# Seventeen groups of edges compared in place of fifteen, layer-norm sums by bn_stats, and earlier first loads in a graph network kernel

## What is computed

```python
h = maximum(layernorm(x), 0)
# three SAGE layers: agg = mean over edges of h[src]; agg @ Wl.T + b + h @ Wr.T, relu after the first two
x = x + sage3(h)
h = maximum(layernorm(x), 0)
messages = gelu((h[src] + edge_attr) @ We1 + be1) @ We2 + be2
aggregated = segment_sum(messages, dst)
x = x + (gelu(((1 + eps) * h + aggregated) @ Wu1 + bu1) @ Wu2 + bu2)
```

## Time and profile before

| | us |
|---|---|
| median of 3 runs (lowest to highest) | 895.88 (895.14 to 899.03) |
| the profiled execution | 895.96 |
| its span, first to last instruction | 894.0 |
| TensorE busy (share of span) | 822.2 (92%) |
| VectorE busy | 662.0 (74%) |
| GpSimd busy | 390.0 (44%) |
| ScalarE busy | 325.3 (36%) |
| mean granted TensorE clock, share of full | 0.974 |

### The profile page before, as it was taken

How to read it: one execution, slowest core, us unless ns; L and a number is a source line. 1 busy time by engine, 2 the same in 40 slices (tenths; PEclk the granted TensorE clock), 3 DMA queues, 4 the chain that set the end, 5 groups by cost and what they waited for, 6 DMA issues and landing times.

```text
span 894.0 us, 14740 instructions
## 1 busy us (share of the span) xinstructions
PE 822.2 (92%) x4894; PEld 626.2 (70%) x4894; DVE 662.0 (74%) x1807; ACT 325.3 (36%) x575; POOL 390.0 (44%) x451
## 2 busy tenths in 40 slices
PE   4987999999999999999699999999899989999995
PEld 1743555555687887778467898887787777888783
DVE  8599999998355445454599988869777877787761
ACT  3576677776155555454111112111112121112111
POOL 1000000000022222232577777777777777777772
PEclk9969999999999999999699999999999999999997
DMA  4300010100000000000673444444434434443421
GB/s 132 86 3 13 3 14 13 15 3 17 9 1 0 1 1 13 12 23 13 149 228 95 126 134 148 135 134 148 127 97 148 136 89 147 135 132 90 136 77 38
DMA packets 37388, 67.50 MB, mean 76 GB/s; under 512 B 14625, under 2 KB 24828, under 8 KB 37180
## 3 DMA queue, kind: packets, MB, share of 16 engines
q1 hardware_dynamic: 25916, 43.15, 16.0%
q0 software_dynamic: 11392, 23.35, 9.6%
HBM read 63.18 MB, written 3.30 MB: 74 GB/s over the span
## 4 chain that ended last, share of the span: by engine, by line
PE 46%; POOL 25%; DVE 15%; issue 10%; DMA 2%; ACT 1%; SPq 0%; ACTq 0%; POOLq 0%; DVEq 0%
POOL f_adj L648 25%; PE f_ps L1332 15%; PE f_ps L1325 9%; DVE f_select L919 4%; PE f_ps L1209 3%; PE f_ps L1387 3%; PE f_ps L1202 3%; PE f_ps L1429 2%; PE f_ps L1299 2%; PE f_ps L1261 1%; PE f_ps L1373 1%; DVE f_region L700 1%; DVE f_region L698 1%; DVE f_adj L1033 1%; DVE f_region L704 1%
## 5 line engine op out<-in xcount | busy, mean ns | idle before, releaser
L648 POOL DMA_INDIRECT f_adj<-table,f_by_edge x356 | 338.3, 950 | 109.8 <-issue 107.0
L919 DVE TENSOR_SCALAR f_select<-f_ps 128x512 fp32r<-128x512 f32 x375 | 230.5, 679 | 3.6 <-PE f_ps L1387 3.1
L1387 PE MATMUL f_ps<-f_select,f_pair 125*128 125x512 f32 x750 | 206.4, 416 | 15.9 <-DVE f_select L919 15.8
L633 POOL CAST f_wide<-f_adj 125x500 fp32r<-125x500 uint8 (+1 forms) x70 | 40.4, 577 | 362.3 <-ACT f_adj L1065 216.4
L1387 PEld LDWEIGHTS f_ps<-f_select,f_pair 125*128 125x128 f32 x750 | 135.6, 190 | 64.3 <-DVE f_select L919 32.2
L1188 ACT ACTIVATE f_adj<-f_adj 128x512 f32<-128x512 f32 (+1 forms) x90 | 56.3, 626 | 326.2 <-DVE f_adj L1033 320.1
L1332 PE MATMUL f_ps<-f_wide,f_pair 125*128 125x500 f32 (+1 forms) x700 | 162.6, 385 | 1.5 <-DVE f_wide L757 0.6
L1065 ACT CAST f_adj<-f_ps 128x500 f32 x213 | 126.1, 592 | 55.7 <-PE f_ps L1209 40.9
L1332 PEld LDWEIGHTS f_ps<-f_wide,f_pair 125*128 125x128 f32 x700 | 122.2, 189 | 33.6 <-issue 6.2
L1429 PEld LDWEIGHTS f_ps<-f_adj 128*128 128x128 f32 x984 | 123.8, 192 | 17.6 <-DVE f_adj L894 8.1
L1429 PE MATMUL f_ps<-f_adj 128*128 128x94 f32 (+20 forms) x984 | 123.8, 271 | 8.8 <-ACT f_adj L1188 8.8
(11 more groups left out here) (147 smaller groups left out, 692.4 us busy)
## 6 DMA issues: line engine op xcount, KB each, us to landing
f_region<-in_edge_attr_T SPq DMA_DIRECT2D x34, 768.0 KB
f_adj<-table,f_by_edge POOLq DMA_INDIRECT x356
f_src_rows<-in_src_row SPq DMA_DIRECT2D x15, 256.0 KB, 4.8
f_adj<-inv SPq DMA_DIRECT2D x1, 1562.5 KB, 7.2
table<-f_region SPq DMA_DIRECT2D x6, 250.0 KB
out<-f_xT SPq DMA_DIRECT2D x6, 250.0 KB, 2.4
f_rcntT<-inv SPq DMA_DIRECT2D x5, 250.0 KB, 3.7
f_xT<-in_xT SPq DMA_DIRECT2D x1, 812.5 KB, 6.2
```

Of the source, the lines that this page charges most:

```text
L648: pool.indirect_dma_start(out=rows[:, r % RW, j * D:(j + 1) * D], out_offset=None, in_=table, in_offset=bass.IndirectOffsetOnAxis(ap=table ...
L919: ins = dve.tensor_scalar(select[:, u % SELECT, :], offset, float(b * NP - CENTRE), None, ALU.is_equal)
L1387: ins = pe.matmul(z_columns(g), chosen[0:NP, p, b, :], select[0:NP, u % SELECT, :], start=b == 0 and p == 0, stop=b == NB - 1 and p == 1, ...
```

## The change

- Seventeen groups are picked (`SHARES`), the gaps between them become six, twice seven.
- The first layer norm's sums come from VectorE: 25 bn_stats in slots 10 to 16 (`statistics0`), joined by five short operations (`join0`) in slot 16, root in slot 17, inversion in slot 20. The products and squares on TensorE and ScalarE go.
- x is loaded ahead of xT, and its loads and the table's stores are cut at partition 112 (`EVENLY`); xT comes later, in one piece, and `dst_tiles` early, straight to where it is used.
- The first edge_attr (three groups) goes to a part of `rcntT` after the fourth table store, the first source row to another part after the fifth; both were issued after the seventh. The rotation of later loads is shifted by one.
- In VectorE's iteration g, the comparisons for g+1 come first, before the one-hots of g+2 and the add of g. On the other engines the order stays.

```diff
-        self.SHARES = 15
+        self.SHARES = 17
...
-            self.put("cent0", 8 + 2 * c, c)
-            self.put("square0", 8 + 2 * c, c)
-            self.put("var0", 10 + 2 * c, c)
+            self.put("stats0", 10 + c, c)
...
-        std = 10 + 2 * s.NC
+        std = 10 + s.NC
+        self.put("join0", std - 1, 0)
         self.put("std0", std, 0)
         self.put("inv0", std + 3, 0)
...
+    EVENLY = NP // 16 * 16
...
         def edge_tiles(g, lo, hi):
             at_tile = s.tile(g) - s.tile(g // PER * PER)
+            if g < PER:
+                return rcntT[:, (at_tile + lo) * P:(at_tile + hi) * P]
             return ea[:, g // PER % EA, (at_tile + lo) * P:(at_tile + hi) * P]
...
-            sp.dma_start(xT[:, 0:HALF * NP], t["xT"][:, 0:HALF * NP]).then_inc(xT_in[0], 16)
-            sp.dma_start(xT[:, HALF * NP:N], t["xT"][:, HALF * NP:N]).then_inc(xT_in[1], 16)
-            sp.dma_start(x_rows[0:NP, 0:HALF, :], t["x"][0:HALF * NP, :].rearrange("(b p) d -> p b d", p=NP)
-                         ).then_inc(x_in[0], 16)
-            sp.dma_start(x_rows[0:NP, HALF:NB, :], t["x"][HALF * NP:N, :].rearrange("(b p) d -> p b d", p=NP)
-                         ).then_inc(x_in[1], 16)
-            sp.wait_ge(x_in[1], 16)
+            for i, (lo, hi) in enumerate(((0, HALF), (HALF, NB))):
+                rows_in = t["x"][lo * NP:hi * NP, :].rearrange("(b p) d -> p b d", p=NP)
+                for p0, p1 in ((0, EVENLY), (EVENLY, NP)):
+                    sp.dma_start(x_rows[p0:p1, lo:hi, :], rows_in[p0:p1, :, :]).then_inc(x_in[i], 16)
+            sp.wait_ge(x_in[1], 32)
...
+            sp.dma_start(xT[:, :], t["xT"]).then_inc(xT_in, 16)
+            sp.dma_start(dst_abs[:, :].bitcast(I32), t["dst_tiles"]).then_inc(dst_tile_in, 16)
...
             for c in range(NC):
...
+                for p0, p1 in ((0, EVENLY), (EVENLY, NP)):
+                    sp.dma_start(rows_to[p0:p1, :, :], rows_from[p0:p1, :, :]).then_inc(rows_out[c % 2], 16)
+                if c == 3:
+                    sp.wait_ge(agg_kept, 2 * NC + 4)
+                    sp.dma_start(rcntT[:, 0:FIRST_EA], t["edge_attr_T"][:, 0:FIRST_EA]).then_inc(ea_first, 16)
+                if c == 4:
+                    sp.wait_ge(agg_kept, 2 * NC + 6)
+                    sp.dma_start(first_src, src_columns(0)).then_inc(src_first, 16)
-            load_edges(0)
-            for i in range(2):
-                sp.dma_start(src_rows[:, i, :], src_columns(i)).then_inc(src_in[i], 16)
-            sp.dma_start(dst_tile[:, :], t["dst_tiles"]).then_inc(dst_tile_in, 16)
+            sp.dma_start(src_rows[:, 1, :], src_columns(1)).then_inc(src_in[1], 16)
...
             load_edges(1)
+            load_edges(2)
...
+            def statistics0(c):
+                for b in s.blocks(c):
+                    if b in (0, HALF):
+                        dve.wait_ge(x_in[b // HALF], 32)
+                    ins = dve.bn_stats(stats0[:, b, :], x_rows[0:NP, b, :])
+                ins.then_inc(stats0_ready, 1)
+
+            def join0():
+                dve.wait_ge(stats0_ready, NC)
+                dve.tensor_tensor(gap0, stats0[:, :, 1], stats0[:, :, 4], ALU.subtract).then_inc(joined0, 1)
+                dve.tensor_tensor(spread0, stats0[:, :, 2], stats0[:, :, 5], ALU.add).then_inc(joined0, 1)
+                dve.tensor_tensor(twice0, stats0[:, :, 1], stats0[:, :, 4], ALU.add).then_inc(joined0, 1)
+                dve.wait_ge(joined0, 3)
+                dve.scalar_tensor_tensor(out=gap0, in0=gap0, scalar=D / 4, in1=gap0, op0=ALU.mult, op1=ALU.mult
+                                         ).then_inc(joined0, 1)
+                dve.wait_ge(joined0, 4)
+                dve.tensor_tensor(spread0, spread0, gap0, ALU.add).then_inc(joined0, 1)
...
                 if g < G:
+                    for i, b in s.selections(g + 1):
+                        select_sources(i, b)
                     if g + OH_AHEAD < G:
                         window_onehots(g + OH_AHEAD)
                     if g not in s.picked:
...
                         dve.tensor_tensor(pre[:, r % PR, 0:w], z_group(g), rows[:, r % RW, 0:w],
                                           ALU.add).then_inc(pre_ready, 1)
-                    for i, b in s.selections(g + 1):
-                        select_sources(i, b)
...
             def root0():
-                act.wait_ge(var0_ready, NC)
-                act.activation(std0[0:NP, :], ps[0:NP, VAR0_PS:VAR0_PS + NB], ACT.Sqrt, bias=col["epsln"][0:NP, 0:1]
+                act.wait_ge(joined0, 5)
+                act.activation(std0[0:NP, :], spread0, ACT.Sqrt, bias=col["epsln"][0:NP, 0:1], scale=1.0 / D
                                ).then_inc(std0_ready, 1)
...
             def mix(g):
-                pe.wait_ge(ea_in[g // PER % EA], 16 * (g // PER // EA + 1))
+                u = g // PER
+                if u == 0:
+                    pe.wait_ge(ea_first, 16)
+                else:
+                    pe.wait_ge(ea_in[u % EA], 16 * ((u + 1) // EA))
```

More of the change, by code:

```diff
@@ L327, in fast_path @@
         rstdT, o = carve(flat, o, (N,), F32)
-        dst_tile, o = carve(flat, o, (FT,), I32)
         uT = rcntT
+        FIRST_EA, FIRST_SRC = PER * T * P, s.cols(4)[0]
+        first_src = rcntT[:, FIRST_SRC:FIRST_SRC + T * P].bitcast(I32)
+        assert FIRST_EA <= s.cols(4)[0] and FIRST_SRC + T * P <= s.cols(5)[1]
         select = placed_at("select", [P, SELECT, T * P], F32R, third)
@@ L340, in fast_path @@
             sem("idx_in"), sem("first_in"), sem("dst_in"), sem("small_in"), sem("sage_in"), sem("gine_in"))
-        x_in, xT_in = [sem(f"x_in{i}") for i in range(2)], [sem(f"xT_in{i}") for i in range(2)]
+        x_in, xT_in = [sem(f"x_in{i}") for i in range(2)], sem("xT_in")
         idx_rest, dst_rest, blank = sem("idx_rest"), sem("dst_rest"), sem("blank")
@@ L345, in fast_path @@
         onehots, nexts_in, summed, kept = sem("onehots"), sem("nexts_in"), sem("summed"), sem("kept")
-        centred0, squared0, var0_ready, std0_ready, scaled0, normed0, hT_kept = (
-            sem("centred0"), sem("squared0"), sem("var0_ready"), sem("std0_ready"), sem("scaled0"), sem("normed0"),
-            sem("hT_kept"))
+        stats0_ready, joined0, std0_ready, scaled0, normed0, hT_kept = (
+            sem("stats0_ready"), sem("joined0"), sem("std0_ready"), sem("scaled0"), sem("normed0"), sem("hT_kept"))
+        stats0 = work[0:NP, 0, 0:6 * NB].rearrange("p (b i) -> p b i", i=6)
+        gap0, spread0, twice0 = (work[0:NP, 1, i * NB:(i + 1) * NB] for i in range(3))
         centred, squared, var_ready, std_ready, inverted, normed = (
@@ L367, in fast_path @@
                                                         sem("selected"))
-        src_in = [sem(f"src_in{i}") for i in range(2)]
-        ea_in = [sem(f"ea_in{i}") for i in range(EA)]
+        src_in, src_first = [sem(f"src_in{i}") for i in range(2)], sem("src_first")
+        ea_in, ea_first = [sem(f"ea_in{i}") for i in range(EA)], sem("ea_first")
         gathered = [sem(f"gathered{i}") for i in range(RW)]
@@ L583, in _ @@
             for g in range(END):
-                if g % PER == PER - 1 and g // PER + EA < UNITS:
+                if g % PER == PER - 1 and EA < g // PER + EA < UNITS:
                     sp.wait_ge(z_ready, g + 1)
@@ L850, in _ @@
                     edge_keys(HEAD, NT)
+                for c in plan.due("stats0", slot):
+                    statistics0(c)
+                for _ in plan.due("join0", slot):
+                    join0()
                 for _ in plan.due("inv0", slot):
@@ L903, in source_offsets @@
                     dve.wait_ge(placed, 2)
[L904 removed]
+                if i == 0:
+                    dve.wait_ge(src_first, 16)
+                else:
+                    dve.wait_ge(src_in[i % 2], 16 * ((i + 1) // 2))
                 if i == 0:
@@ L1147, in _ @@
                     root0()
-                for c in plan.due("square0", slot):
-                    square0(c)
                 for c in plan.due("square", slot):
@@ L1211, in sum_group @@
                 ins.then_inc(summed, 1)
-            def centre0(c):
-                if c == 0:
-                    pe.wait_ge(xT_in[0], 16)
-                if s.blocks(c)[-1] >= HALF > s.blocks(c)[-1] - s.NBC:
-                    pe.wait_ge(xT_in[1], 16)
-                if c >= 2:
-                    pe.wait_ge(squared0, c - 1)
-                pe.matmul(ps[:, cent0_ps(c):cent0_ps(c) + width(c)], cent[:, :], at(xT, c), start=True, stop=True
-                          ).then_inc(centred0, 1)
-                for b in s.blocks(c):
-                    pe.matmul(ps[0:NP, MEAN0_PS + b:MEAN0_PS + b + 1], xT[:, b * NP:(b + 1) * NP], mean[:, 0:1],
-                              start=True, stop=True)
-            def variance0(c):
-                lo, hi = s.cols(c)
-                pe.wait_ge(squared0, c + 1)
-                for b in s.blocks(c):
```

(7 more changed lines are left out.)

35 lines of the change are left out of this document (11 added, 24 removed).

## The result

The changed kernel takes 911.16 us (median of 4, 909.71 to 912.08), beside 896.07 for the kernel before (median of 4): a ratio of 1.0149, 95% interval 1.0107 to 1.019. It is slower, as forecast (905), by 1.5%; the time stands 0.2 above the range given for 8 in 10, which ended at 911, and inside the forecast's own range, 894 to 915. The profiled execution has a span of 909.4.

What follows compares the result with a forecast made beforehand. Gathers bound the edge stage with TensorE close behind; the change makes TensorE the bound: 510.0 + 298.8 + 51.8 + 22.5 + 24.5 = 907.6, less 4.0 for the first stage; forecast 905, 8-in-10 range 881 to 911, own range 894 to 915.

Steps and rivals of the forecast that it cites:

- First layer norm: First stage: VectorE's bn_stats put the first normalisation at 43.8 where it stood at 47.79, a gain of 4.0 us.
- Rival 3: First stage: bn_stats are dear or x is late, losing up to 5.8 us where 4.0 gained was counted; chance 0.15.
- First loads: Edge stage start: edge_attr, first src row and dst on chip early let VectorE start its first offsets 6.8 us earlier.
- GpSimd: Edge stage: eight gathers fewer at 1.25 us each save 10.0 us.
- The loop: Edge stage: TensorE product, units, comparisons, add, product again take 5.73 us against TensorE's 4.56; stands 1.17, twice per six-group gap.
- The gap: Edge stage, one picked group's turning-back to the next: six groups take 22.6 us of TensorE work plus 2.3 standing, 24.9.
- Boundaries: Edge stage: five node block boundaries add 5.9 us each, 1.4 of it fitting into idle time: 4.5 each, 22.5 together.
- third turning back: Edge stage: TensorE's turning-back of the third picked group, put at 510.0 before subtracting 4.0 for the first stage.
- tail: End of the kernel, 868.08 to 894.0 before: 25.9 us less 1.44 waiting for a gather, 24.5.
- the gathers' end: Edge stage rival: TensorE and VectorE keep up, gathers still set the end, span 880 and time 882; chance 0.30.
- The condition that the prediction named: Edge stage sign against the prediction: VectorE finishes comparisons before TensorE reaches the iteration, so the chain of waits does not close.
- Rival 2: Edge stage: TensorE's boundary work halves the waiting cost, 23.8 us per gap of six, about 894, no change; chance 0.20.

## Why the prediction was nearly right

- **First layer norm.** Predicted first normalisation 43.8, measured 43.95. A bn_stats is 0.195 from start to start (four in a slot add 0.78 to its 0.76: 20.69 to 22.23), not 0.26, so 1.6 us cheaper over 25. Two things that the sum left out took this back: the inversion's wait of 0.98 for ScalarE's root, and a one-hot operation of 675 columns (L734 at 35.55), 0.78 until the next instruction. That the sum came out to 0.15 is luck. Rival 3 fell; it stood close, for without the cut 5.05 us are lost.
- **First loads.** First offsets predicted at 429, measured at 429.03. The sum counts them in full since it forecast a TensorE-bound stage; in a kernel with the loop open up to 3.7 us of them is worth nothing.
- **GpSimd.** Predicted 10.0 saved. From fifteen to seventeen, order behind the add, the last gather moves from 874.3 to 866.2: 8.1. Where the rest went was not traced.
- **The loop.** Predicted 5.73, measured 5.78. TensorE's work in a gap: predicted 22.6, 22.56 with the loop open. The gap: predicted 24.9, measured 25.05, 25.04 and 25.06 in the three gaps that touch no boundary. So a gap of six pays 2.49 where the sum had 2.3, and one of seven 1.68 where it had 1.5. Ten and six buffers confirm the terms: 22.73, and a loop of 6.97 against 6.94.
- **Boundaries: the mis-sized term.** From the third turning back to the last the sum had 373.1, and it took 379.4. With the order turned back that stretch is 354.8, less what the last gap waits behind a gather 352.6. Twelve gaps of 22.56 and two of 24.3 (one product and one sum more) leave 33.3 for boundaries, where the sum had 29.5 (five of 5.9). The 5.9 was read from the first boundary alone, which takes 5.8 here; the five take 5.8, 7.3 (1.26 of it a wait for ScalarE, at 605.60), 5.9, 6.5 and 6.7, and 1.0 of a sixth falls into the last gap. Set gap by gap beside that kernel, the changed one is 26.8 longer in all: 33.2 for the loop in all gaps (12 x 2.49 + 2 x 1.68), less 6.4 where boundary work fits into its idle time (the sum had 7.0): four gaps of six pay only 0.7, 0.7, 1.3 and 0.7. So the boundaries cost 26.9 net where the sum had 22.5. The loop's 33.2 are 2.6 over the sum's 30.6, and the gaps' own work gives back 0.7: 4.4 + 2.6 - 0.7 is the 6.3.
- **Third turning back and tail.** 508.1 for 506, 21.9 for 24.5. With the order turned back the third turning back stands at 503.12, so the order costs 5.0 up to there where the sum had 2.5. The tail was not traced. That the two nearly cancel is luck.

The errors add to the 5.8 us between the sum's span (903.6) and the measured one: 2.1 + 6.3 - 2.6. Of the rivals, the gathers' end (882) is what the kernel does once the loop is open: 883.28, 882.97 and 883.54. The condition that the prediction named, whether "VectorE gets its comparisons done before TensorE reaches the iteration", is the one that decides: two more buffers, or the order, meet it. Rival 2 had the loop's cost absorbed by half at the boundaries; a fifth of it was. Its sum also slipped: twelve gaps of 23.8 in place of 24.9 take 13.2 from 907.6, which leaves 894.4, not 895.6.

## What to carry to other kernels

When an instruction that waits for a ring's buffers is put ahead of one that feeds the ring's consumer, follow the chain once around: consumer, buffer, waiting instruction, what stands behind it, consumer again. If the sum is longer than the consumer's own iteration, the order costs the difference each time, and opening the loop at any one place (order, or as many buffers as put its sum below the iteration) gives it back: all 28 us here by the order, 24 to 25 by the buffers. With the loop open by the order, more buffers give nothing. Where two engines are close to being the bound, moving work from one to the other pays only to the crossing: here the two groups up to seventeen bring 9 us (892.25 to 883.28), and the eighteenth costs 12 (10 of them in the span).

## What the runs showed of the hardware

Two figures I had not expected. Four bn_stats of 125x128 f32 take 0.86 us, where four operations that write a result of that shape took 1.13. And longer stands of TensorE went with a lower clock. In the changed kernel it stood about 1.0 us for the add at a time, and the granted clock was 1.00 over 511 to 890; with six buffers it was 0.97 over 511 to 946. There TensorE stood 2.2 us for the add fourteen times. After seven of these stands the granted clock fell to 0.50 (1.2 GHz of 2.4) for about 3 us, as at 739; after the other seven (582.98 and 589.95 are two) it did not, and an eighth fall, at 612, followed a stand of 1.37. Both the single stands and their sum are larger with six buffers (55.2 us against 20.6), so what decides stays open.
